# Layer norm factors by ln and exp on ScalarE, an earlier table load, and a router weight by exp, in a hybrid scan and expert kernel

## The reference

```python
x = x + ln_gb(s6(ln(x)) @ Wo + bo + ln(x))      # selective scan, 256 inner channels, 64 states each
x = x + moe(ln(x))                              # 8 experts, top 2, hidden 256
x = x + s5(ln(x))                               # diagonal complex scan, 64 states
x = x + moe(ln(x))
# s6: h = exp(delta * A) * h + delta * B_t * x_t ;  y_t = C_t * sum(h)
# moe: top_w = softmax(top 2 of x @ Wg);  out = sum over the two of top_w * (silu(x W1) * (x W2)) @ W3
```

## Time and profile before

| | |
|---|---|
| median of 3 runs | 1848.97 us |
| the profiled execution | 1861.63 us |
| its span | 1859.7 us |
| turns 3 to 5, from mid to mid | 214.9, 211.7, 211.7 us |
| VectorE, GpSimd, TensorE, ScalarE busy | 1514.5, 1513.9, 1351.0, 1281.5 us |

### The profile page before, as it was taken

The page is one execution under the profiler, slowest core; times in us unless marked ns, Lnnn a source line. Parts: engine busy times, 40 slices in busy tenths (PEclk is TensorE's granted clock), DMA queues, the critical chain, the costliest instruction groups (busy, mean ns, idle before and its releaser), DMA issues.

```text
span 1859.7 us, 19053 instructions
## 1 busy us (share of the span) xinstructions
PE 1351.0 (73%) x5928; PEld 617.7 (33%) x5928; DVE 1514.5 (81%) x2105; ACT 1281.5 (69%) x2275; POOL 1513.9 (81%) x888
## 2 busy tenths in 40 slices
PE   4336458777886887778776878778787778668958
PEld 1001123234342343324342343324332343324535
DVE  4879988898889889898899888888888988895222
ACT  4547668687877778777777778777787777755423
POOL 0899999978998799977998899987998799983312
PEclk9557569889987989879897989879898898979979
DMA  3601411122111311132101401132111321100000
GB/s 87 212 34 71 164 46 51 49 91 97 57 40 48 148 51 33 54 104 96 55 25 50 162 29 51 49 106 81 51 51 49 102 85 52 46 29 1 7 1 6
DMA packets 38747, 121.89 MB, mean 66 GB/s; under 512 B 5875, under 2 KB 21110, under 8 KB 26358
## 3 DMA queue, kind: packets, MB, share of 16 engines
q1 hardware_dynamic: 37062, 120.67, 18.3%
q10 hardware_dynamic: 1584, 0.01, 0.0%
HBM read 109.13 MB, written 11.53 MB: 65 GB/s over the span
## 4 chain that ended last, share of the span: by engine, by line
PE 27%; ACT 18%; DVE 15%; POOL 14%; issue 8%; DVEq 0%; POOLq 0%; ACTq 0%
DVE h L1251 10%; POOL w L947 9%; PE bankH L565 8%; ACT da L837 5%; PE bankY L579 5%; PE bankG L565 5%; ACT yk L798 4%; ACT L837 3%; PE ys L633 2%; POOL x L890 2%; PE bankG L512 2%; DVE aq L1189 1%; PE bankY L559 1%; ACT L785 1%; ACT sq L785 1%
## 5 line engine op out<-in xcount | busy, mean ns | idle before, releaser
L1251 DVE TENSOR_TENSOR_SCAN h<-da,w 128x512 f32<-128x512 f32 x1024 | 1192.1, 1206 | 158.3 <-ACT da L837 133.0
L947 POOL TENSOR_TENSOR w<-ur,br 128x1024 f32<-128x1024 f32 x512 | 1193.6, 2365 | 33.1 <-DVE h L1251 21.2
L837 ACT ACTIVATE da<-dr,al 128x511 f32<-128x511 f32 x1024 | 681.9, 687 | 221.9 <-DVE h L1251 212.5
L633 PE MATMUL ys<-h,wsum 128*32 128x512 f32 x2048 | 320.9, 703 | 208.5 <-DVE h L1251 189.2
L565 PE MATMUL bankH<-nT,w 128*128 128x512 f32 x512 | 301.8, 673 | 89.7 <-DVE aq L1189 85.3
L890 POOL TENSOR_TENSOR x<-x,yk 128x512 f32<-128x512 f32 x128 | 163.1, 1274 | 211.2 <-ACT yk L798 210.6
L579 PEld LDWEIGHTS bankY<-w,aq 128*128 128x128 f32 x2048 | 262.8, 203 | 87.0 <-issue 65.0
L579 PE MATMUL bankY<-w,aq 128*128 128x128 f32 x2048 | 270.5, 289 | 12.4 <-DVE aq L1189 7.9
L565 PE MATMUL bankG<-nT,w 128*128 128x512 f32 x432 | 243.8, 648 | 24.6 <-DVE aq L1189 24.6
L798 ACT ACTIVATE yk<-bankY,rt 128x128 f32<-128x128 f32 x512 | 151.8, 364 | 121.5 <-PE bankY L579 107.8
L633 PEld LDWEIGHTS ys<-h,wsum 128*32 128x32 f32 x2048 | 42.9, 115 | 408.5 <-DVE h L1251 373.2
(11 more groups left out here) (187 smaller groups left out, 1135.8 us busy)
## 6 DMA issues: line engine op xcount, KB each, us to landing
br<-b_rows SPq DMA_DIRECT2D x64, 1024.0 KB, 5.0
dr<-d_rows SPq DMA_DIRECT2D x16, 1024.0 KB, 7.1
ur<-u_rows SPq DMA_DIRECT2D x16, 1024.0 KB, 8.4
d_rows<-vh SPq DMA_DIRECT2D x16, 256.0 KB
u_rows<-th SPq DMA_DIRECT2D x16, 256.0 KB
xnew<-in_L_attn_a_x_dram SPq DMA_DIRECT2D x8, 256.0 KB, 5.3
w<-in_L_ffn_W_dram SPq DMA_DIRECT2D x2, 1024.0 KB, 11.1
x<-in_L_attn_a_x_dram SPq DMA_DIRECT2D x8, 256.0 KB, 9.1
```

Of the source, the lines that this page charges most:

```text
L633: ins = nc.tensor.matmul(ys[32 * q:32 * q + 32, :], wsum[:, :], h[:, (DUOS * t.b + 2 * group + q // 2) % H_RING, q % 2, :], start=(n == 0) ...
L837: A(da[duo % D_RING][:, k % 2, 1:L], dr[:, half, q, 1:L], ACT.Exp, scale=nega[:, QUADS * half + q, n:n + 1]).then_inc(decay_ready, 1)
L947: G.tensor_tensor(w[:, turn_duo % W_RING, :, :], ur[:, half, q:q + 2, :], br[:, chunk % B_RING, row:row + 1, :].to_broadcast([128, 2, L]), ...
L1251: V.tensor_tensor_scan(h[:, turn_duo % H_RING, k % 2, :], da[duo % D_RING][:, k % 2, :], w[:, turn_duo % W_RING, k % 2, :], 0.0, ALU.mult, ...
```

## The change

Norms 1, 2 and 4 get their factor elsewhere, in the turns that scan (`t.scans`: 0 to 7). ScalarE makes `rs` as exp(-0.5 * ln(variance + eps)) five slots behind the moments; VectorE makes `nm` in one instruction three slots behind the moments, and waits for ScalarE's Exp there; ScalarE's norm waits for `nm`. GpSimd makes nothing for these norms. The load of `DECAYS` follows directly behind the fourth silu of each block except the last one of the first experts. The router's weight is 1 / (1 + exp(gap)), with two more small VectorE instructions behind the gap and one fewer before it, and it is no longer doubled; W3 is left as it is. In the tail the norms stay on GpSimd and the gap's tanh stays.

```diff
-SCALE_AT = 52
-RSTD_LAG, NORM_LAG = 6, 6
-ROUTE = 14
+RSTD_LAG, NORM_LAG, ROOT_LAG, SHIFT_LAG = 6, 6, 5, 3
+ON_SCALAR = (1, 2, 4)
+ROUTE, LAST_ROUTE = 15, 14
...
-            def normalize(k, i, at, src, dst):
+            def normalize(k, i, at, src, dst, here=False):
+                if here:
+                    yield at + ROOT_LAG
+                    act.wait_ge(moments_ready[k], 4 * i + 4)
+                    A(rs[:, k, :], bag[:, k, :, 1], ACT.Ln, bias=eps[:, 0:1]).then_inc(rstd_ready[k], 1)
+                    act.wait_ge(rstd_ready[k], 2 * i + 1)
+                    A(rs[:, k, :], rs[:, k, :], ACT.Exp, scale=-0.5).then_inc(rstd_ready[k], 1)
                 yield at + NORM_LAG + (2 if k == 2 else 0)
-                act.wait_ge(rstd_ready[k], 4 * i + 4)
+                if here:
+                    act.wait_ge(shift_ready[k], i + 1)
+                else:
+                    act.wait_ge(rstd_ready[k], (2 if k in ON_SCALAR else 4) * i + 4)
...
                         A(zt[j % 4], p[:, :], ACT.Silu).then_inc(drained[BANK[f"h{m}_{j}"]], 1)
+                        if j % 4 == 3 and t.scans and (m, j) != (1, 2 * E - 1):
+                            act.preload_act_table_set(DECAYS)
                     elif name == "gap":
-                        A(rc[:, 2, :], rc[:, 3, :], ACT.Tanh, scale=0.5).then_inc(gap_tanh_ready, 1)
+                        if t.scans:
+                            A(rc[:, 2, :], rc[:, 3, :], ACT.Exp).then_inc(gap_weight_ready, 1)
+                        else:
+                            A(rc[:, 2, :], rc[:, 3, :], ACT.Tanh, scale=0.5).then_inc(gap_weight_ready, 1)
...
-            def rstd(k, i, at):
+            def rstd(k, i, at, elsewhere=False):
                 yield at
+                if elsewhere:
+                    return
...
-                for n in range(QUADS):
-                    yield SCALE_AT + 3 * n
-                    if n == 0:
-                        pool.wait_ge(expert_loads, 16 * EXPERT_LOADS)
-                    part = w3[:, 2 * n:2 * n + 2, :, :].rearrange("p e k c -> p (e k c)")
-                    G.tensor_scalar(part, part, 0.5, None, ALU.mult).then_inc(outputs_scaled, 1)
...
-            def moments(k, i, at, src):
+            def moments(k, i, at, src, shift=False):
...
+                if shift:
+                    yield at + SHIFT_LAG
+                    v.wait_ge(rstd_ready[k], 2 * i + 2)
+                    V.scalar_tensor_tensor(nm[:, k, :], bag[:, k, :, 0], -1.0, rs[:, k, :], ALU.mult, ALU.mult).then_inc(shift_ready[k], 1)
...
+                def weight():
+                    if t.scans:
+                        link(V.tensor_scalar(rc[:, 2, :], rc[:, 2, :], 1.0, None, ALU.add))
+                        link(V.reciprocal(rc[:, 2, :], rc[:, 2, :]))
+                    else:
+                        link(V.tensor_scalar(rc[:, 2, :], rc[:, 2, :], -0.5, 0.5, ALU.mult, ALU.add))
...
-                link(V.tensor_tensor(R(4), R(2), R(1), ALU.subtract))
-                link(V.tensor_tensor(R(5), R(2), R(1), ALU.add))
+                link(V.tensor_tensor(R(5), R(1), R(2), ALU.subtract))
                 yield SLOT[f"lg{m}"] + 5
-                v.wait_ge(gap_tanh_ready, 2 * c + m)
-                link(V.tensor_tensor(R(4), R(4), spread(rc[:, 2, :]), ALU.mult))
-                drain(f"lg{m}", V.tensor_tensor(rt[:, 0, :, :], R(4), R(5), ALU.add))
+                v.wait_ge(gap_weight_ready, 2 * c + m)
+                weight()
+                link(V.tensor_tensor(R(5), R(5), spread(rc[:, 2, :]), ALU.mult))
+                drain(f"lg{m}", V.tensor_tensor(rt[:, 0, :, :], R(5), R(2), ALU.add))
```

More of the change, by code:

```diff
@@ L176, in __init__ @@
         self.b, self.on, self.done = b, {"pre": pre, "post": post, "late": late}, {"pre": pres, "post": posts, "late": lates}
-        self.pre, self.post, self.late = pre, post, late
+        self.pre, self.post, self.late, self.scans = pre, post, late, 0 <= b < NB
     def begin(self, bank):
@@ L291, in hybrid_kernel @@
         stats_ready = [sem(f"stats_ready{k}") for k in range(5)]; moments_ready = [sem(f"moments_ready{k}") for k in range(5)]
[L292 removed]
+        rstd_ready = [sem(f"rstd_ready{k}") for k in range(5)]; shift_ready = [sem(f"shift_ready{k}") for k in range(5)]; normed = [sem(f"normed{k}") for k in range(5)]
         tanh_ready = sem("tanh_ready"); biased_ready = sem("biased_ready"); abs_ready = sem("abs_ready"); relu_ready = sem("relu_ready"); exp_ready = sem("exp_ready"); log_ready = sem("log_ready")
@@ L805, in post @@
                 c = t.b - 1
-                yield from normalize(1, c, LN_AT[1], z, nrm)
-                yield from normalize(2, c, LN_AT[2], x1, nrm)
+                yield from normalize(1, c, LN_AT[1], z, nrm, t.scans)
+                yield from normalize(2, c, LN_AT[2], x1, nrm, t.scans)
                 yield from moe(t, 1, False)
@@ L811, in post @@
                 copy_out(t, "uT", nT[:, :])
-                yield from normalize(4, c, LN_AT[4], x2, nrm)
+                yield from normalize(4, c, LN_AT[4], x2, nrm, t.scans)
                 yield from moe(t, 2, False)
@@ L893, in post @@
                 c = t.b - 1
-                yield from rstd(1, c, LN_AT[1] + RSTD_LAG)
+                yield from rstd(1, c, LN_AT[1] + RSTD_LAG, t.scans)
                 pool.wait_ge(residual_in, 16 * c + 16)
@@ L902, in post @@
                 G.tensor_tensor(x1[:, :, :], nrm[:, :, :], x1[:, :, :], ALU.add).then_inc(x1_ready, 1)
-                yield from rstd(2, c, LN_AT[2] + RSTD_LAG)
+                yield from rstd(2, c, LN_AT[2] + RSTD_LAG, t.scans)
                 yield from expert_sums(t, 1, False)
                 yield from rstd(3, c, LN_AT[3] + RSTD_LAG)
-                yield from rstd(4, c, LN_AT[4] + RSTD_LAG)
+                yield from rstd(4, c, LN_AT[4] + RSTD_LAG, t.scans)
                 yield from expert_sums(t, 2, False)
@@ L948, in pair @@
                                     br[:, chunk % B_RING, row:row + 1, :].to_broadcast([128, 2, L]), ALU.mult).then_inc(product_ready, 1)
-                weave(pair, [gates(t)] + ([scale_outputs()] if known(t.b, 1) else []) + tasks_of(t, pre_a, post, late))
+                weave(pair, [gates(t)] + tasks_of(t, pre_a, post, late))
             turns(pre_a, scan, post, late)
@@ L1141, in routing @@
                 done = [0]
-                r0 = ROUTE * (2 * c + m - 1)
+                route = ROUTE if t.scans else LAST_ROUTE
+                r0 = ROUTE * 2 * c + route * (m - 1)
                 def link(ins):
@@ L1199, in post @@
                 v.wait_ge(drained[BANK["z"]], t.before("z") + 1)
-                yield from moments(1, c, LN_AT[1], z)
+                yield from moments(1, c, LN_AT[1], z, t.scans)
                 yield LN_AT[2]
                 v.wait_ge(x1_ready, c + 1)
-                yield from moments(2, c, LN_AT[2], x1)
+                yield from moments(2, c, LN_AT[2], x1, t.scans)
                 yield from both(moe_tiles(t, 1, False), routing(t, 1))
@@ L1234, in post @@
                 v.wait_ge(drained[BANK["s5t"]], t.before("s5t") + 1)
-                yield from moments(4, c, LN_AT[4], x2)
+                yield from moments(4, c, LN_AT[4], x2, t.scans)
                 yield from both(moe_tiles(t, 2, False), routing(t, 2))
```

16 lines of the change are left out of this document (7 added, 9 removed).

## The result

The changed kernel takes **1874.1 us** in the median (1873.2 to 1875.7, four runs), the kernel before 1852.7 us beside it (1846.1 to 1856.9, four runs). The ratio is **1.0112, 95% interval 1.0081 to 1.0143**: 21 us slower, where 11 us faster was forecast, and above the upper end of the range (1853).

What follows compares the result with a forecast made beforehand. VectorE and GpSimd were level and neither full, so only VectorE's waits for GpSimd counted. Turn 0 -6.1, turn 1 0.0, turns 2 to 6 -4.4, turn 7 -0.8: -11.3 off 1849.0 gives 1837.7 us, range 1816 to 1853.

Steps and rivals of the forecast that it cites:

- The router: Each routing: one operation fewer before the gap, hidden; two small ones more behind it, +0.43 us each routing, +0.86 per turn.
- early loads: Decays' table load directly behind the fourth silu fills ScalarE's idle time at slot 3: -1.15 us per turn, turns 2 to 7.
- Turn 0, -6.1: Turn 0: four W3 scalings of 1528 ns leave GpSimd, which is the bound there: -6.1 us, bounds -6.1 and -3.
- Norm 2, -1.94 per turn: After the residual: GpSimd without the factors covers scan waits of 0.75 and 1.19 us, -1.94 us per full turn.
- The shift: VectorE's new 128x4 instruction per norm, three slots behind the moments: 0.2 us, plus any wait for ScalarE's Exp.
- Norm 1, +0.45: Ln and Exp on ScalarE stand before the silu block that holds the scans 3.82 us: +0.45 us, fully exposed.
- Norm 4, +0.7: Behind the softplus and decays: VectorE waits 0.5 us for the factor and works 0.2 us, +0.7 us.
- The norms as a whole: Factors of norms 1, 2 and 4 leave GpSimd; full-turn terms -1.94, +0.45, +0.2 and +0.7 us.
- Rival 3: Slower: VectorE's wait for ScalarE's Exp closes a ring through GpSimd's sum at norm 2; +12, 1861 us; chance 0.10.
- Rival 4: An Exp reloads its own set behind each early load, 1.28 us per block, +64 us over 50 blocks; chance 0.02.
- Rival 1: GpSimd's lateness costs more than the places counted; full turn -3.4 us, in all -30, 1819 us; chance 0.22.
- Wrong if full turns move by more than 2 us: Sign against the forecast, which had full turns near 210.8 us instead of 211.7.

Runs made afterwards that it cites:

- clean exp router: Changed kernel with 1+exp(gap) and the difference of the two choices kept in PSUM instead of SBUF: 1855.8 us, 1.0023 to the kernel before.
- tanh router: Changed kernel with the router of the kernel before (tanh, 0.5 folded into two existing operations, W3 unscaled): 1825.2 us, 0.9866 to the kernel before.
- the dummy in SBUF: Kernel before plus one unread 128x4 add, SBUF to SBUF, in each routing behind the wait for the gap: 1888.7 us, 1.0179.

## Why the prediction was wrong, step by step

- **The router: the step that failed.** It was priced at two operations 0.23 us apart, 0.43 us for each routing, 0.86 per turn, 6 us in all. It cost 31 + 16.5 us. (On the kernel with W3 unscaled the clean exp router costs nearly the same, 0.0161 or 30 us. In the kernels with early loads and the norms on GpSimd it costs nothing, 1.0018 against 1.0011, but there the tanh has 14 more table loads.) The duration came from L1174 and L1175, both of which read PSUM; the new add goes from SBUF to SBUF, its multiply reads two SBUF tiles. The nearest row was near in size, not in operands. The Trainium skill has the rule, on the page "SBUF — State Buffer", section "Who interferes with whom": a VectorE operation of a two-port mode (a plain tensor_scalar can be one) or with two SBUF inputs contends with GpSimd's for one shared pair of ports, which the first one keeps for its whole instruction. The runs agree on which operations are held (SBUF to SBUF 1188 ns, to PSUM 156) and show a longer hold than one instruction: 4.50 us, where one product takes 2.32. The prediction didn't hold the router's operands against this rule. The other 31 us are no duration either: the two operations are busy for 4.7 us, but a full turn with them takes 211.5 us at a mean clock of 0.90, without them 208.2 at 0.92.
- **No term for the clock: the sum's other gap.** The prediction added and took off work at places. 0.2 us at one place measured 19 us, and the early loads, priced at 7 us, measured +7, -22 or -54 by the kernel around them. My own rows showed two kinds of full turn in the kernel before (214.85 and 211.7), and I took neither as a warning.
- **Turn 0, -6.1: right.** It ends at 213.99 us instead of 219.72, -5.7, of which 1.1 lies ahead of the first scan, where the executions differ anyway (it starts between 51.0 and 55.5 us in all traces); W3 unscaled alone gives 0.0026, 5 us.
- **Norm 2, -1.94 per turn: the mechanism right,** and the size near (16 us in seven turns, measured on the tanh router). The waits of 0.75 and 1.19 are gone, seven scans run on end, and ScalarE's wait for GpSimd's sum is 0.39 instead of 1.46:

```profile
888.81 0.63 ACT L810 ACTIVATE yk<-bankY,rt 128x128 f32<-128x128 f32 x2 [0.39 <-POOL x L896]
...
890.42 0.63 DVE L1110 SCALAR_TENSOR_TENSOR nm<-bag,rs 128x4 f32<-128x4 f32 x1
...
894.94 7.88 DVE L1269 TENSOR_TENSOR_SCAN h<-da,w 128x512 f32<-128x512 f32 x7
```

  The shift was to take 0.2 us and takes 0.63 beside GpSimd's products. It, too, has two SBUF inputs. In turn 1 it takes 2.82.
- **Norm 1, +0.45:** the scan behind its silu block waits 4.07 us instead of 3.82, +0.25. **Norm 4, +0.7: wrong in the good direction.** The factor is out in time, and the shift takes 0.13 us with no wait; the stretch gained 0.5 us where 0.7 + 0.43 were to be lost. Norms 1 and 4 together, counted as costs, gave 11 us on the tanh router.
- **The early load: the place right, the price wrong.** At slot 3 it now fills TensorE's time, and neither the weighing behind it waits (1.19 before) nor the scan (1.11 before):

```profile
858.44 0.60 ACT L792 ACTIVATE sq<-bankG 128x512 f32<-128x512 f32 x1 [0.36 <-PE bankG L565]
859.05 1.28 ACT L794 ACT_TABLE_LOAD   x1
860.35 0.63 ACT L810 ACTIVATE yk<-bankY,rt 128x128 f32<-128x128 f32 x2
```

  But in the same place VectorE now waits 2.90 us for TensorE instead of 1.21, so the 1.15 were lost again to the lower clock. And the step has no one price: on the tanh router it cost 7 us (with 14 more loads), on the clean exp router it gave 22, with as many loads as without it, and with the norms on ScalarE 0.0294 of the ratio, 54 us, where ln and exp find one common set loaded: their own loads fall from 26 to 2, while the tanh's 14 come. A load is again followed by work at once, at 860.35, so here too there is no sign of the drain that the Trainium skill's page "ScalarE: Activation LUTs", section "What ACT_TABLE_LOAD costs", counts.
- **The norms as a whole** were to give some 4 us. On the tanh router they gave 0.0145 of the ratio, 27 us, in a kernel that had the early loads, on the clean exp router nothing (1.0018 and 1.0023). So its value depends on the kernel around it. The runs show that the good turns have TensorE at the higher clock, that they are 3.3 us shorter with nearly the same work of the other engines, and that the clock falls before the time is lost; which shift tips which stretch stays open.
- **Rivals.** Rival 3, the ring of waits, didn't occur: 1.9 us in all for 21 shifts. Rival 4 neither (one load more for ln, one for exp). Both appear together as soon as the early loads are taken out. Rival 1's time, 1819, was closest to what the change does without its router (1825, 1827), but its mechanism was not tested, so this may be luck. None of my cases contained the one that happened, an operation held by the other engine; the slow side ended at a 0.12 chance for a mechanism that this kernel avoids.
- **"Wrong if full turns move by more than 2 us":** they moved by 3.4.

## What to carry to other kernels

Before a small operation is priced from a row of the trace, compare operands as well as size: an add from SBUF to SBUF, or a multiply of two SBUF inputs, took up to 4.5 us instead of 0.2 beside a GpSimd that runs without a pause. Keep the add's output, or one of the two inputs, in PSUM, as the kernel before did throughout its router. In a kernel like this one, whose TensorE changes its clock several times in every turn, look at the clock of the turns before believing a sum of small terms: one operation of 0.2 us per routing cost 19 us of 1830. Price parts in the kernel that they will run in, not one by one: the early loads cost 7 us in one, gave 22 in another and 54 in a third.

## What the hardware showed that I had not expected

- A held VectorE operation doesn't always get in when GpSimd's current instruction ends: 4.50 us against products of 2.32 us each, back to back; 2.82 us in turn 1, over two products. Yet the shift at 890.42 got through in 0.63. All held ones, here and in the kernel with the dummy in SBUF, end within 0.05 us of the end of a GpSimd product; of that dummy's 14 held ones 12 got in at the first such end, two at the second. What decides between them was not tried.
- With the decays' set loaded early, the router's tanh needs a load of its own. It had none before, since the set loaded behind the tiles then held it:

```profile
L797 ACT ACT_TABLE_LOAD x14 | 18.0, 1283 | 0.2
```

  Yet the kernel with these 18 us of loads (1825) is no slower than the one without (1827): ScalarE has the room there, and VectorE had none for 0.2 us.
- Runs of one kernel sort by clock in part. Of twelve runs of the kernel with W3 unscaled, nine at mean granted clocks of 0.871 and 0.872 took 1842.3 to 1844.5 us, two at 0.860 took 1852. The profile on which the prediction rests had 0.860 and 1861.6 us, where the kernel before mostly runs at 0.866 to 0.874. But the mean doesn't tell all: at 0.870 and 0.871 the kernel before took from 1845.1 to 1858.6 us.
